# The fifth early group's residual: accumulating stores instead of loads, VectorE adds and plain stores

## The reference

```python
x = x + _layernorm(_L0_attn_ref(_layernorm(x), ...))          # call the result x2
x = x + _layernorm(_L0_ffn_ref(_layernorm(x), gate_w, w1, b1, w2, b2,
                               shared_w1, shared_b1, shared_w2, shared_b2))
# _L0_ffn_ref: the two best of 8 experts for each token, weighted, plus a shared
# expert gelu(n @ shared_w1 + shared_b1) @ shared_w2 + shared_b2
```

## Time and profile before

| | us |
|---|---|
| median of 3 runs | 904.56 |
| lowest and highest | 904.41 and 906.53 |
| the profiled execution's own time | 903.74 |
| its span, first to last instruction | 901.9 |

### The profile page before, as it was taken

How to read it: one execution, slowest core, us unless ns; L and a number is a source line. 1 busy time by engine, 2 the same in 40 slices (tenths; PEclk the granted TensorE clock), 3 DMA queues, 4 the chain that set the end, 5 groups by cost and what they waited for, 6 DMA issues and landing times.

```text
span 901.9 us, 14793 instructions
## 1 busy us (share of the span) xinstructions
PE 850.7 (94%) x4510; PEld 712.6 (79%) x4510; DVE 671.6 (74%) x1446; ACT 430.1 (48%) x815; POOL 404.5 (45%) x322
## 2 busy tenths in 40 slices
PE   4999999999999989999999885999999999999986
PEld 3888888878888778788888664888888888888865
DVE  6977989889879887687778596566666656665877
ACT  5235445336242243242413471566666666666564
POOL 1457567576565010000001001567677667762275
PEclk9999999999999999999999988999999999999998
DMA  9228878778749798758533988588888879888999
GB/s 322 98 104 314 296 263 328 268 284 315 252 158 401 309 382 308 288 209 324 187 129 102 398 324 264 107 220 166 142 142 170 197 155 166 148 136 203 370 250 220
DMA packets 88026, 212.30 MB, mean 235 GB/s; under 512 B 11576, under 2 KB 20024, under 8 KB 82576
## 3 DMA queue, kind: packets, MB, share of 16 engines
q1 hardware_dynamic: 63520, 166.61, 50.6%
q0 software_dynamic: 19360, 43.60, 26.3%
q10 hardware_dynamic: 5072, 1.15, 0.8%
HBM read 118.23 MB, written 93.11 MB: 234 GB/s over the span
## 4 chain that ended last, share of the span: by engine, by line
PE 55%; DVE 19%; issue 8%; DMA 6%; ACT 6%; POOL 5%; DVEq 0%; POOLq 0%; SPq 0%; ACTq 0%
PE bank L1671 6%; PE bank L1672 6%; PE bank L1673 6%; PE bank L1916 4%; PE bank L1901 4%; PE bank L1915 3%; PE bank L1914 3%; PE bank L1933 3%; PE bank L1931 3%; PE bank L1932 3%; DMA n_scratch<-picked 2%; DVE rot L976 2%; PE bank L1666 2%; PE bank L1923 2%; POOL rsn L1548 2%
## 5 line engine op out<-in xcount | busy, mean ns | idle before, releaser
L1614 POOL DMA_INDIRECT f_scratch<-ro,dst x71 | 112.5, 1585 | 54.5 <-SPq L602 24.7
L1606 POOL DMA_INDIRECT xr<-n_scratch,ids x71 | 70.2, 989 | 71.9 <-issue 44.1
L1408 DVE TENSOR_TENSOR ro<-bank,b2b 128x512 f32<-128x512 f32 x71 | 49.1, 692 | 67.6 <-PE bank L1933 55.7
L1671 PE MATMUL bank<-wkv_hi,h_hi 128*128 128x512 f32 x248 | 97.2, 392 | 0.0
L1673 PE MATMUL bank<-wkv_hi,h_lo 128*128 128x512 f32 x248 | 96.6, 389 | 0.0
L1672 PE MATMUL bank<-wkv_lo,h_hi 128*128 128x512 f32 x248 | 96.5, 389 | 0.0
L1914 PE MATMUL bank<-we,x_hi 128*128 x284 | 86.1, 303 | 0.5 <-DVE x_lo L1383 0.5
L667 ACT ACTIVATE sq<-kb 128x512 f32<-128x512 f32 x32 | 20.3, 634 | 130.1 <-DVE kb L979 130.1
L1916 PE MATMUL bank<-we,x_lo 128*128 x284 | 80.4, 283 | 0.0
L1915 PE MATMUL bank<-we,x_hi 128*128 x284 | 80.4, 283 | 0.0
L1541 POOL TENSOR_TENSOR acc<-acc,prod 128x512 f32<-128x512 f32 x32 | 57.6, 1798 | 8.7 <-DVE prod L992 8.7
(11 more groups left out here) (248 smaller groups left out, 2490.7 us busy)
## 6 DMA issues: line engine op xcount, KB each, us to landing
xg<-in_X SPq DMA_DIRECT2D x15, 1024.0 KB, 7.9
we<-expert_scratch SPq DMA_DIRECT2D x6, 2048.0 KB, 13.6
w_lo<-in_w SPq DMA_DIRECT2D x16, 512.0 KB, 5.5
expert_scratch<-w_hi SPq DMA_DIRECT2D x16, 512.0 KB, 2.8
expert_scratch<-w_lo SPq DMA_DIRECT2D x16, 512.0 KB, 4.2
q_scratch<-qh SPq DMA_DIRECT2D x8, 1024.0 KB, 3.9
q_scratch<-qb SPq DMA_DIRECT2D x8, 1024.0 KB, 6.1
q_hi<-q_scratch SPq DMA_DIRECT2D x8, 1024.0 KB, 4.8
```

Source lines behind the costliest of these rows:

```text
L1606: pool.indirect_dma_start(xr[u][:, :], None, n3_dram, bass.IndirectOffsetOnAxis(ids[:, i:i + 1], 0)).then_inc(row_in[u], 16)
L1614: pool.indirect_dma_start(f_dram, bass.IndirectOffsetOnAxis(dst[:, i:i + 1], 0), ro[i % NRO][:, :], None, compute_op=ALU.add).then_inc(r_s ...
L1671: pe.matmul(dst, hi(k), w_hi(k), start=(k == 0), stop=False)
```

## The change

`ADDED` becomes empty, and `x2c` of group 5 keeps its place at 136 KB.

```diff
-        ADDED = EARLY[4:]
-        x2c = {g: at(f"x2c{g}", kb_, [P, GT, D]) for g, kb_ in zip(ADDED + LATE[-1:], (128, 136))}
+        ADDED = EARLY[5:]
+        x2c = {g: at(f"x2c{g}", kb_, [P, GT, D]) for g, kb_ in zip(ADDED + LATE[-1:], (136,))}
```

## The result

| | us |
|---|---|
| kernel before, median of 8 runs | 904.77 |
| changed kernel, median of 8 runs | 908.47 (907.04 to 911.46) |
| ratio, 95% interval | 1.0041 (1.0025 to 1.0058) |
| its profiled execution, and its span | 911.46, 909.2 |

The change costs 0.41%, 3.7 us. The forecast was +0.17%, with 0.18 on slower by over 0.3%; the direction and the mechanism were right, the size was less than half of what came, and a result slower by over 0.3% had been given less than one chance in five.

What follows compares the result with a forecast made beforehand. VectorE's chain and the DMA drain end side by side. Backlog gone at 899.3 + 2.9 + 0.67 - 0.3 + 0.5 + 0.45 gives span 903.45, 1.55 us more; on the median 906.1 us (+0.17%), range 903.6 to 908.6.

Steps and rivals of the forecast that it cites:

- Part 1: VectorE's tail: four additions leave, some 2.6 us, but TensorE is late next; -0.4 us if nothing else held the end.
- Part 2: Load of 1 MB on q1, 844 to 858 us, goes: 0 to 2.7 us of credit at the end, taken as 0.3.
- Part 3: DMA queues, 885 to 899 us: four plain stores become accumulating, 1.39 against 0.67 us each, +2.9 us in all.
- the sum: DMA backlog's end at 899.3 us plus store costs, less load credit, plus landing and closing: span 903.45, +1.55 us.
- Part 4: POOL's list in the tail: four more issues at 0.89 us each stay hidden, with 0.9 and 1.4 us to spare.
- the prediction's own formula: POOL's tail: time from 885.11 to the needed root at 892.5, less 1.14, over six issues: 1.05 us each.
- Rival C: POOL's in-order list delays the roots of (5,1) and (5,2), from 1.06 us an issue; up to 910.4 us; chance 0.15.
- A: The forecast itself: the DMA queues' drain takes the end over from VectorE, 906.1 us; chance 0.57.
- + 0.45 as before: End of program: the span ends 0.45 us behind the last store's landing, as in the kernel before.
- Rival B: Tail: drain hidden by the whole 2.7 us load credit or cheap accumulating stores; VectorE's gain shows, 904.2 us; chance 0.28.

Runs made afterwards that it cites:

- The dose series: Kernel before (24 accumulating stores) varied to 20, 28 (the change) and 32, VectorE adding the rest: +0.16%, +0.33 to +0.41%, +0.84% against it.
- the second profile: The changed kernel run again, unchanged, beside the kernel before: 910.23 us, ratio 1.0033; 29.6 us from the mark to the end.

## Why the prediction was right where it was, and where it failed

**What bounds the kernel.** Right: VectorE's chain and the queues' drain end side by side, and the first work added to the queues showed in the time. The dose series has its kink at the kernel before.

**Part 1, VectorE.** Right. 0.34 us of lateness at (5,3) are gone (0.41 to 0.07), and taking all of part 1 and 2 away without a price gives 0.4 us in the profile. What was late next was TensorE.

**Part 2, the load.** Taken at 0.3 us of credit, because the queue was to be nearly dry at 884 us. Putting a load back did not change the ratio, so little or nothing of the 2.7 us reached the end. The reason is not shown: 131 GB/s in that slice stood beside a DMA share of 1.05, which doesn't say that the queue was short of work. A share of up to 1 us is left open.

**Part 3, the price of the stores.** The price was right, the landing came out later than the sum has it. From 887.4 to 901 us the changed kernel's q0 runs nearly alone:

```profile
q0 software_dynamic: 1445, 2.63, 110.9%
q1 hardware_dynamic: 14, 0.03, 0.6%
```

2.63 MB in 13.6 us is 1.36 us for a store of 0.262 MB, where I had 1.39. The landing of the last store came out 1.5 and 1.7 us later from the mark, against 1.55 in the sum. That agreement is not like with like, since only the kernel before had the dip; the one profile of the changed stores that has it too, with the load kept, lands its last store at 29.0 us from the mark, 2.8 later than before. Like with like it moved further: 25.9 us with the four stores plain to 29.0 with them accumulating and the load kept, both with the dip, 3.1 us; 25.6 us with the old stores and one issued last to 27.9 and 27.7 in the change, none with the dip, 2.1 to 2.3 us. So some 0.5 us or more of landing may be missing in the sum as well; which of its terms that is stays open.

**Part 4, POOL.** The price was wrong, and the conclusion held narrowly. The issue records grew far beyond the 0.89 us of the sum, up to 3.30 us, and the root of (5,1) took 2.65 us:

```profile
892.44 2.65 POOL L1643 TENSOR_TENSOR fr<-fv,half 128x1 f32<-128x1 f32 x1
```

VectorE used it at 895.13, some 0.1 to 0.2 us late, and took (5,3) in time all the same. By the prediction's sign (line 1460 waits for POOL behind 892 us) part 4 was wrong. The records overlap, though, so their length is not the pace: from the first of these issues, at 887.53, to the end of that root is 7.56 us, and by the prediction's own formula, (7.56 - 1.14)/6, that is 1.07 us an issue, against 1.05 as the point at which C decides. Rival C had the right place and was just at its point; it did not decide. That the long records come from the queue's backlog is what the run with plain stores speaks for.

**The range.** The measured 908.47 us lies 0.13 us inside its upper end, 908.6. A's own upper bound was 908.0; the rest had been added for C, which is not what happened. That the range holds the result is luck.

**The step that failed is the last term of the sum: "+ 0.45 as before" from the last landing to the end of the span.** It was read off a kernel in which POOL's DRAIN was done before SP and was carried over to one in which it is last. It measured 2.0 us (907.2 to 909.2), and 1.9 in the second profile. The missing 1.5 us and the forecast 1.55 make 3.1 us; 3.0 and 3.3 were measured from the mark, and the timed ratios are +3.0 and +3.7 us. That this sum comes out is in part chance: the kernel before has the dip and the change has not, and like with like the landing alone moved by 2.1 us or more (part 3). For the warning sign the rows of before would have done: DRAIN on POOL, 5.15 us long, ended 2.5 us behind the landing of POOL's last store (891.1 + 7.3 = 898.4), only 0.6 us ahead of SP. I had read the waits of the engines and the DMA queues, but not the closing instructions.

**Rival B** would have needed the credit for the load whole, which the run with a load kept speaks against, or an accumulating store at about the price of a plain one. The two rates refute the second, and so does the run in which only the accumulation was taken away: 0.43 to 0.51% lower. The fit of the Trainium skill in DMA: Bandwidth & Descriptors, Anatomy of one DMA (2.0 us plus bytes at 436 GB/s), does not describe these stores: at 0.193 MB in a us they move at less than half of that rate.

## What to carry to other kernels

Before moving an addition off a compute engine onto accumulating stores, price the store by the queue's own rows: here it took the 16 DMA engines 1.36 us where a plain one took about 0.67 (an estimate from the earlier trace rows), while the addition it replaced lay almost wholly in TensorE's shadow. Here the work that was added where the DMA engines are full cost its whole price, and the load that was removed ahead of the tail gave back little or nothing. List every end that the program waits for, the closing DRAIN of each engine among them, with its distance to the last one: a term that is hidden by 0.6 us today is the next bound tomorrow.

## What the runs showed of the hardware

- POOL's closing DRAIN ended 2.3 to 2.9 us behind the landing of its last transfer in all nine profiles: 900.9 behind 898.4 before, 909.0 behind 893.6 + 12.8 = 906.4 in the change, 905.6 behind 903.2 with one store issued last, 911.6 behind 908.8 with nothing added by VectorE, 905.2 behind 895.4 + 7.5 = 902.9 with groups 6 and 7 added. In the kernel whose last POOL store was plain it was 2.7 (902.7, the last one issued at 893.4 and landed 6.6 us later), so it doesn't come from the accumulation.
- An issue on POOL is not of fixed length. It took 0.88 us where it stood alone (891.11 before, with the DMA engines full) and up to 3.3 us with a backlog of some nine stores (my estimate: 12.8 us to landing, at 1.36 us each), and roots issued beside it stretched from 0.57 to 2.65 us.
- The tail's queue does not seem to follow TensorE's clock. In the stretch that begins 8.5 us ahead of the last product's end, q0 had 1.80 MB left in the kernel before, where the clock had been at half for some 3 us, and 2.10 MB in the kernel with one store issued last, where it had not. Of one profile each, this speaks for it that a tail that the compute engines finish sooner leaves more of the stores for the end.
